# A Mamba-2 scan whose x is turned and weighed later in each step

## The reference

```python
proj = hidden_states @ W_in.T                    # z, x, B, C, dt
xBC = silu(causal_conv(xBC, 4 taps))
x_dt = x * dt[..., None]                         # 64 heads of 64 channels
Y_diag = einsum('bclhn,bcshn,bhcls,bcshp->bclhp', C_c, B_c, Lmat, x_dt)
states = einsum('bclhn,bhcl,bclhp->bchpn', B_c, decay_states, x_dt)
new    = prev * exp(d_k)[..., None, None] + s_k  # from chunk to chunk
Y_off  = einsum('bclhn,bhcpn,bhcl->bclhp', C_c, prev_states, exp(A_cum))
y = (Y_diag + Y_off) + D_param[..., None] * x
g = y * silu(z);  out = (g * rsqrt(mean(g*g)) * norm_w) @ W_out.T
```

## Time and profile before

| what | value |
|---|---|
| median of 3 runs | 3499.25 us (3494.03 to 3501.69) |
| the profiled execution's own time | 3496.68 us |
| its span, first to last instruction | 3494.8 us |
| TensorE (PE) busy | 3356.3 us, 96% |
| VectorE (DVE) busy | 2682.2 us, 77% |
| ScalarE (ACT) busy | 2107.7 us, 60% |
| GpSimd (POOL) busy | 881.4 us, 25% |
| first and last turn of x in the scan (L1888) | 1612.7 and 3092.3 us |

### The profile page before, as it was taken

One profiled execution on the slowest core, in us unless ns is written; L12 is line 12 of the kernel. 1 busy time (PEld: TensorE's weight loads), 2 busy tenths in 40 slices (PEclk: granted clock), 3 DMA queues, 4 the chain that ended last, 5 costly groups with the idle time before them and its releaser, 6 DMA issues. The chain is left out here.

```text
span 3494.8 us, 58291 instructions
## 1 busy us (share of the span) xinstructions
PE 3356.3 (96%) x20672; PEld 2369.3 (68%) x20672; DVE 2682.2 (77%) x5227; ACT 2107.7 (60%) x3380; POOL 881.4 (25%) x819
## 2 busy tenths in 40 slices
PE   9899999999999888988999999999999999999998
PEld 7644444444444477766777777777777777778886
DVE  4577777777777485567999989999999899975443
ACT  3156656656666733445777777777777777763332
POOL 0012222222222300002344433443444334430000
PEclk9999999999999999999999999999999999999999
DMA  7333443443442311247666766677667866640100
GB/s 247 79 86 92 110 92 92 110 92 92 110 92 74 124 46 36 77 156 233 233 226 228 253 232 231 226 261 240 227 218 246 280 221 234 230 157 28 37 13 25
DMA packets 264224, 531.43 MB, mean 152 GB/s; under 512 B 32000, under 2 KB 54656, under 8 KB 260736
## 3 DMA queue, kind: packets, MB, share of 16 engines
q1 hardware_dynamic: 263936, 527.71, 47.5%
HBM read 430.60 MB, written 96.47 MB: 151 GB/s over the span
## 5 line engine op out<-in xcount | busy, mean ns | idle before, releaser
L628 ACT ACTIVATE probs<-prob_scores 128x1024 f32<-128x1024 f32 (+3 forms) x640 | 572.4, 896 | 380.5 <-PE prob_scores L560 372.6
L583 PE MATMUL times_v<-probs,VS 128*64 128x256 f32 (+2 forms) x4608 | 612.2, 382 | 17.5 <-ACT outT L662 12.6
L684 DVE TENSOR_REDUCE part_max<-ring 128x1 f32<-128x512 f32 x720 | 463.1, 685 | 112.3 <-PE ring L552 110.8
L49 PE MATMUL bank<-QS,KS 128*128 128x512 f32 x1024 | 452.6, 442 | 13.3 <-ACT sc_xr L1999 6.2
L583 PEld LDWEIGHTS times_v<-probs,VS 128*64 128x64 f32 x4608 | 279.6, 136 | 256.4 <-issue 161.0
L51 PE MATMUL bank<-QS 128*128 128x512 f32 x1024 | 403.4, 394 | 0.0
L50 PE MATMUL bank<-KS,QS 128*128 128x512 f32 x1024 | 401.5, 392 | 0.0
L1850 POOL TENSOR_TENSOR sc_xdd<-sc_xdt,sc_small 128x512 f32<-128x512 f32 x128 | 244.8, 1912 | 565.5 <-DVE sc_xdt L2121 565.5
L2022 ACT ACTIVATE sc_M<-sc_later,sc_small 128x128 f32<-128x128 f32 x1024 | 311.8, 389 | 0.0
L560 PE MATMUL prob_scores<-QS,KS 50*128 50x512 f32 (+3 forms) x1280 | 298.2, 462 | 3.7 <-PEq L142 1.9
L2112 DVE SCALAR_TENSOR_TENSOR masked_scores<-sc_xr,sc_chan,masked_scores 128x512 f32<-128x512 f32 x384 | 290.9, 758 | 13.6
(11 more groups left out here) (374 smaller groups left out, 7159.5 us busy)
## 6 DMA issues: line engine op xcount, KB each, us to landing
sc_later<-scan_acum SPq DMA_DIRECT2D x128, 512.0 KB, 4.7
sc_ce<-scan_expa SPq DMA_DIRECT2D x128, 512.0 KB, 5.3
QS<-scan_W_high SPq DMA_DIRECT2D x252, 256.0 KB, 2.8
KS<-scan_W_low SPq DMA_DIRECT2D x252, 256.0 KB, 3.5
sc_woh<-scan_Wo_high SPq DMA_DIRECT2D x128, 256.0 KB, 4.1
sc_wol<-scan_Wo_low SPq DMA_DIRECT2D x128, 256.0 KB, 4.9
w_raw<-in_Wg SPq DMA_DIRECT2D x64, 256.0 KB, 2.9
scan_W_high<-w_hi SPq DMA_DIRECT2D x64, 256.0 KB, 2.0
```

The source lines that it names most:

```text
L49: pe.matmul(out, ll, rh, start=start, stop=False)
L583: mm = pe.matmul(po[MV * s:MV * (s + 1), CHUNK - w + n * h:CHUNK - w + (n + 1) * h], VS[p % 2][:, j, :], PT[u % NPT][:, s, n * h:(n + 1) * ...
L628: act.activation(PT[u % NPT][:, :, 0:w], pb[u % 2][:, :, 0:w], ACT.Exp).then_inc(exped, 1)
L684: dve.tensor_reduce(to, slot(n)[:, 0:w], AX.X, ALU.max).then_inc(emptied, 1)
```

## The change

On TensorE `turn_x(t + 1)` moves from the head of step t to behind `outputs(t)` and `states(t)`. On VectorE `weigh_x(t + 1)` moves from the head of the step to behind `next_state(t)`, so that `weigh_c(t + 1)` is first. No instruction is added or removed, no buffer and no wait is changed; GpSimd's, ScalarE's and SyncE's lists stay as they are.

```diff
                 turn_x(0)
                 for t in range(STEPS):
+                    outputs(t)
+                    states(t)
                     if t + 1 < STEPS:
                         turn_x(t + 1)
-                    outputs(t)
-                    states(t)
                     mine = tiles_in(t)
                     for n in mine[:EARLY[t % QT]]:
                         project_in(n)
...
                 for t in range(STEPS):
                     if t + 1 < STEPS:
-                        weigh_x(t + 1)
                         weigh_c(t + 1)
                     gate(t)
                     next_state(t)
                     if t + 1 < STEPS:
+                        weigh_x(t + 1)
                         weigh_decays(t + 1)
                     rest(t)
```

## The result

The changed kernel takes 3506.3 us (median of 21 runs, 3501.41 to 3512.8); the kernel before took 3498.93 on the same chip (21 runs, 3494.03 to 3504.08). The medians lie 7.4 us apart, and the ratio is 1.0022, with a 95% interval of 1.0016 to 1.0028: slower, at the edge of what I had called no change (7 us). I had forecast 3504 us, in a range of 3490 to 3530. The time is right. What follows looks at whether its terms were.

What follows compares the result with a forecast made beforehand. TensorE's own work was taken as the bound; terms 0 - 2.5 + 2 + 5 + 0 = +4.5 us took the profiled 3496.68 to 3501.2, and 2.6 us up to the median gave 3504 us, range 3490 to 3530.

Steps and rivals of the forecast that it cites:

- What bounds the kernel: Whole scan: TensorE's own work sets the end, PE busy for all of a 46.78 us block; waits offer a few us.
- Rival B: Step c2: DVE becomes the bound, blocks of 47.5 us or more with M waits; 3510 to 3545 us, chance 0.33.
- rival C: TensorE loads the outputs' weights ahead, so blocks fall under 46.5 us; 3489 us or less, chance 0.11.
- Rival D: Nothing moves: DVE's collisions stay hidden and the waits are too small; 3499 us, chance 0.02.
- TensorE's order: Around the turn's place: 0.44 us a step saved behind L51, 0.44 lost behind states; 0, bounds 15 us faster, 13 slower.
- Waits for SiLU: The turn's wait for SiLU, 3.7 us in 9 waits, goes as the turn moves later; -2.5 us, between -0.9 and -3.7.
- Turns of DVE and POOL: Scan steps: SBUF instructions of both engines run in turns, xdd now meeting M and rest; DVE's block becomes 46.85 us.
- Regular blocks: 24 blocks: c2's deadline holds by 0.5 us, drift of 0.07 a block uses it up; +2 us, bounds 0 and +87.
- Row updates: Last quarter, four blocks with a 1.87 us row update on DVE in c2: missed deadlines, +5 us, bounds 0 and 7.5.
- The last steps: Last four steps, no projections, DVE-bound: xdd already meets gate's product there; 0, between -2 and +2 us.
- reload: Reload of x by DMA behind the last projection of the old x: the same TensorE work lies between; 0.

Runs made afterwards that it cites:

- experiment 4: Changed kernel with weigh_x put between gate and next_state on VectorE, against the changed kernel: 3505.64 us.
- Experiment 5: Changed kernel with POOL's xdd product done on 8 of its 512 columns only, against the changed kernel: 3498.97 us.
- experiment 8: Changed order up to step 123, the order before in the last four steps (both engines), against the changed kernel: 3503.46 us, one run.

## Why the prediction was right, and which terms were not

**What bounds the kernel.** Right: PE's own work sets the end, and the block is 46.76 us. Rival B (blocks of 47.5 us or more) and rival C (under 46.5) both failed. In c0 the two engines took turns in the order that I had worked out, and no block before the row updates shows the loss that B priced for POOL keeping its turn in c2 and c3. Rival D's 3499 us did not come either.

**TensorE's order, taken as 0: about -0.7 us.** PEld around the new place of the turn:

```profile
1912.54 0.19 PEld L51 LDWEIGHTS bank<-QS 128*128 128x128 f32 x1
1913.08 0.20 PEld L1902 LDWEIGHTS bank<-sc_M,sc_xdt 128*64 128x64 f32 x4 [0.35 <-issue]
...
1914.98 0.30 PEld L1912 LDWEIGHTS bank<-sc_xdd,sc_B 128*128 128x128 f32 x2 [0.17 <-issue]
1915.52 0.14 PEld L1888 LDWEIGHTS bank<-ident,sc_xT 128*128 128x128 f32 x1 [0.24 <-issue]
1915.95 0.36 PEld L1888 LDWEIGHTS bank<-ident,sc_xT 128*128 128x128 f32 x3 [0.29 <-issue]
1916.27 0.19 PEld L49 LDWEIGHTS bank<-QS,KS 128*128 128x128 f32 x1
1916.38 0.19 PEld L50 LDWEIGHTS bank<-KS,QS 128*128 128x128 f32 x1
```

The same place in the kernel before, without the turn:

```profile
1915.37 0.30 PEld L1912 LDWEIGHTS bank<-sc_xdd,sc_B 128*128 128x128 f32 x2 [0.17 <-issue]
...
1916.34 0.19 PEld L50 LDWEIGHTS bank<-KS,QS 128*128 128x128 f32 x1 [0.24 <-issue]
```

L51 to L1902 is 1913.08 - 1912.54 = 0.54 us, the value that I had borrowed from the earlier trace rows. The profile puts the gap in the earlier trace rows down to a wait for DVE, which I hadn't weighed; here the same gap stands with no wait. Behind the states the four transposes cost 1.40 us from L1912 to L50, where before it was 0.97: 0.43, and I had 0.44. The whole detour saved some 0.005 us a step. The two ends of the bounds, 15 us faster and 13 slower, were both far off, and the row from another stage was the right one to go by. The first load of the other shape starts 0.35 us after the load before it has ended, the same gap as in the earlier trace rows, so the earlier load across shapes that rival C needed isn't seen. The Trainium skill (TensorE: Matmul & The Clock Gate, Step-by-step) says that a load may be pulled ahead of running products; no run here shows that across shapes.

**Waits for SiLU, -2.5: -2.1.** They show as c2 steps of 11.70 us where before had 11.96 (steps 30 and 62), 11.86 (94), 12.02 (106), and as 1.13 us in step 122. What stays of them is 1.7 us in seven short waits, part of the gaps above.

**Turns of DVE and POOL.** Right in mechanism, and most single lengths hold: `rest` 1.54 (1.5), the copy 1.25 (1.3), M in c2 with 0.64 us to spare (0.5). M in c1 came at 6.73 us into its step (7.1). What I had missed is the second copy, 0.97 us.

**Regular blocks, +2: 0.** The slack of 0.5 that I expected to drift away stayed at 0.64. The drift was 0.07 us a block in a sum of some 30 lengths, and the sum was 0.54 us too long. DVE at the end of the block, after:

```profile
1945.54 0.69 DVE L2169 TENSOR_TENSOR sc_acc<-sc_acc,bank 128x512 f32<-128x512 f32 x1 [0.45 <-PE bank L51]
1946.14 1.22 DVE L2127 TENSOR_TENSOR sc_ce<-sc_ce,sc_C 128x1024 f32<-128x1024 f32 x1
```

From `ce` to the next block's `ce` go 1946.14 - 1899.38 = 46.76 us, and 0.45 of them are a wait for TensorE: DVE's own block is 46.31 us, where I had 46.85. c0 and c1 take 15.53 and 15.64 (15.47 and 15.7 in the sum); c2 and c3 together take 15.14 and not 15.68. So DVE still ends each block waiting for TensorE, and nothing can drift. M in c1 also still waits 0.72 us for ScalarE's Exp, which I had taken as just ready. A drift of the kind that I feared shows in experiment 4.

**Row updates, +5: +4.2.** Before, a c2 step with a row update was 11.71 us; here the lengths are 12.22, 12.21, 12.24 and 12.61, and c3 behind them 9.29, 9.30, 9.51 and 9.28 where 8.94 is free of waits. Less the 1.5 us of SiLU waits and the 0.1 of TensorE's order that go in the same steps this is the +2.6 of the window. I had expected a wait of 1.4 us in each block; two blocks lose 0.5 in c2 and 0.35 in c3, 0.9 in all, the third 1.1 and the last 1.25. The rest stays with DVE as backlog, as M's slack in c2 shows, which is 0.05 from step 110 on. Experiment 5 has none of it.

**The last steps, 0 between -2 and +2: +4.5.** This is the mis-sized term, and the reason is in two sentences of the prediction. I wrote that these steps have no projections and that `xdd` meets the gate's product there already, and so left them out. But I let the row updates leave a backlog and didn't carry it on. DVE in step 124, which begins at 3080.83, and in 125, which begins at 3090.12:

```profile
3082.75 2.09 DVE L2187 TENSOR_SCALAR w<-w,sc_rows_mv,sc_ln 128x512 f32<-128x512 f32 x2
3084.76 1.21 DVE L2127 TENSOR_TENSOR sc_ce<-sc_ce,sc_C 128x1024 f32<-128x1024 f32 x1
...
3087.65 0.68 DVE L2138 TENSOR_TENSOR sc_state<-later_keys,bank 128x512 f32<-128x512 f32 x1
...
3088.85 1.22 DVE L2132 TENSOR_TENSOR sc_M<-sc_M,sc_CB 128x1024 f32<-128x1024 f32 x1
...
3096.67 0.69 DVE L2138 TENSOR_TENSOR sc_state<-later_keys,bank 128x512 f32<-128x512 f32 x1 [1.00 <-POOL later_keys L1864]
```

`ce`, the first instruction of the step on DVE, starts 3.93 us into it; before, `xdt` started 1.19 us into its step. M for step 124 had 2.36 us of slack before and has 0.05 now, and from it to the next M, which ends at 3090.07, go 9.29 us instead of 8.86. The 2.3 of backlog and the 0.4 are the 2.7 us by which step 124 is longer (9.29 instead of 6.56).

Steps 125 and 126 are longer by 0.7 and 1.05, and there the cause is another one, which the prediction didn't list. In the last group POOL has three small sums behind `ssq`. POOL from step 125 on, and DVE's next sum of the state:

```profile
3092.73 2.38 POOL L1878 TENSOR_TENSOR sc_ssq<-sc_ssq 128x128 f32<-128x128 f32 x3
3095.07 1.49 POOL L1864 TENSOR_TENSOR later_keys<-sc_state,sc_small 128x512 f32<-128x512 f32 x1
```

```profile
3106.06 0.69 DVE L2138 TENSOR_TENSOR sc_state<-later_keys,bank 128x512 f32<-128x512 f32 x1 [1.36 <-POOL later_keys L1864]
```

The sum of the state waits 1.00 us in step 125 and 1.36 in 126 for POOL's `sd`. The late order closes a ring here: `xdt` stands behind the state's sum, `xdd` behind `xdt`, then on POOL `ssq`, the three sums and `sd`, and the next state's sum behind `sd`. From state's sum to state's sum go 3096.67 - 3087.65 = 9.02 us and 3106.06 - 3096.67 = 9.39, the lengths of steps 125 and 126. With `xdt` ahead of the state's sum there is no such ring: before, experiment 8 and experiment 4 have no wait for `sd` in these steps. In experiment 4 `xdd` still meets M, and yet steps 125 and 126 take 16.57 us together, before 16.68 and after 18.41. So the 1.9 us of the last steps' own order are in the main this ring. The turns make it longer (`sd` takes 1.49 us in it and 1.04 in the c0 shown above), and a short `xdd` makes it shorter; how much of it is turns no run parts.

In step 125 TensorE also runs slower. For the 3.1 us ahead of its outputs it has next to nothing to do (windows before and behind their start):

```profile
3087.00:3090.12 3.12, 0.09 (x1) 0.00 (x1) 3.08 (x6) 2.35 (x7) 1.11 (x1) 1.00 0.66 215
3090.12:3094.00 3.88, 3.88 (x33) 3.52 (x34) 3.82 (x4) 2.19 (x5) 3.80 (x3) 0.56 1.02 327
```

The granted clock is 0.56 over the stretch, near the lower level of 1.2 GHz, and from the outputs to the states go 3093.68 - 3090.12 = 3.56 us instead of 1.90. The step isn't longer for it: the product of the states ends near 3094.81, and the state's sum waits until `sd` has ended at 3096.56. In experiment 8 step 125 is 0.34 us longer than before at a lowered clock, and step 126 is 0.35 shorter, so its 2.6 us are backlog and not the clock.

**The time.** The sum in the profile was +4.5 and the measured span is +6.4. The misses of -2 (regular blocks), -0.8 (row updates), -0.7 (TensorE's order), +0.4 (SiLU), +0.8 (reload) and +4.5 (last steps) partly cancel: the total is better than its parts, and that is luck.

## What to carry to other kernels

An instruction moved on one engine moves its consumers too. Here a product on GpSimd, hidden beside VectorE work that reads PSUM, came to lie beside work on SBUF only, and such a meeting costs VectorE what is left of the other's turn: here `rest` took 1.54 us beside a product of 512 columns and 0.70 beside one of 8. Look at the smallest slack before a deadline, not at the mean of busy time: 2.1 us of slack paid for this for 26 blocks. Then look for the stretches where extra work (row updates) or less cover (the steps without projections) meets the backlog, and carry it across their border. Look also whether the consumer of the moved instruction leads back to it in the next step: such a ring has a length of its own. And two edits that belong together can each be bad alone: neither half tells what the whole does.

## Not expected

A GpSimd product of 8 columns took 1.13 us beside M, more than half of the 1.96 of one with 512. It ended 0.07 us behind M's end, so even the short one waited for the VectorE instruction. Its successors on VectorE pay little for it, though (`rest` 0.70). And 3.1 us nearly without a product were followed by a granted clock of 0.56 over 3.9 us, where the block and the steps 104 to 123 have 1.00.
